# A ring of channel pairs in the mixing stages of a four-layer pairwise network on one Trainium2 core

## The reference

```
x = x + L0(gn(x));  x = x + L1(gn(x));  x = x + L2(gn(x));  x = x + L3(gn(x))

L0: a, b = sigmoid((x@Wa1+ba1)*(x@Wa2+ba2)), the same with Wb      (16 channels each)
    z = einsum('bikc,bkjc->bijc', a, b)                             (16 mixed channels)
    out = sigmoid(x@Wg+bg) * (ln(z)@Wz+bz)
L1: h = (ln(x)@pi+..)*sigmoid(ln(x)@gi+..) * mask;  a1,b1,a2,b2 = split(h, 4)
    z = concat(einsum('bikd,bjkd->bijd', a1, b1), einsum('bkid,bkjd->bijd', a2, b2))   (16 + 16)
    out = (ln(z)@po+..) * sigmoid(ln(z)@go+..)
L2: a, b = split(p_in*sigmoid(g_in), 2);  z = einsum('bikc,bjkc->bijc', a, b)          (64)
    out = (ln(z)@p_out) * sigmoid(ln(x)@g_out)
L3: left, right gated and multiplied by m[i]*m[k];  z = einsum('bkid,bkjd->bijd', left, right)  (64)
    out = (ln(z)*gate)@W_out + b_out
```

## Time and profile before

| | |
|---|---|
| median of 3 runs | 1714.95 us |
| the profiled execution | 1716.62 us |
| its span in the trace | 1714.7 us, 26817 instructions |
| PE busy | 1435.4 us (84%) |
| DVE busy | 1172.3 us (68%) |
| ACT busy | 1050.5 us (61%) |
| POOL busy | 429.0 us (25%) |
| DMA | 381.51 MB, mean 222 GB/s |

### The profile page before, as it was taken

How to read it: one execution, slowest core, us unless ns; L and a number is a source line. 1 busy time by engine, 2 the same in 40 slices (tenths; PEclk the granted TensorE clock), 3 DMA queues, 4 the chain that set the end, 5 groups by cost and what they waited for, 6 DMA issues and landing times. The chain is left out here.

```text
span 1714.7 us, 26817 instructions
## 1 busy us (share of the span) xinstructions
PE 1435.4 (84%) x9119; PEld 750.9 (44%) x9119; DVE 1172.3 (68%) x2060; ACT 1050.5 (61%) x1845; POOL 429.0 (25%) x382
## 2 busy tenths in 40 slices
PE   5796697968587697899979997998899967785987
PEld 5535432212376242133338996222233336663443
DVE  5643587179688884289957777893499956677664
ACT  4674686844234786688856666556688834444555
POOL 5400197130000594310000000792500000000665
PEclk9898899989898898999989998998899989997999
DMA  8336310026657230079987886891088878785998
GB/s 341 105 153 225 143 54 9 1 87 194 213 205 278 99 99 13 1 270 345 344 315 298 302 302 235 303 378 51 26 343 341 345 272 319 305 305 198 375 393 314
DMA packets 140872, 381.51 MB, mean 222 GB/s; under 512 B 13505, under 2 KB 13634, under 8 KB 130626
## 3 DMA queue, kind: packets, MB, share of 16 engines
q1 hardware_dynamic: 118418, 314.95, 50.4%
q10 hardware_dynamic: 22320, 64.86, 10.1%
HBM read 191.01 MB, written 188.74 MB: 221 GB/s over the span
## 5 line engine op out<-in xcount | busy, mean ns | idle before, releaser
L1350 POOL TENSOR_TENSOR xT<-xT,work 128x512 f32<-128x512 f32 x192 | 241.7, 1277 | 700.6 <-DVE work L1395 698.2
L1046 PE MATMUL bank<-work 128*128 128x256 f32 x1408 | 349.3, 401 | 59.4 <-DVE work L1112 23.9
L746 ACT ACTIVATE work<-bank,bias 128x512 f32<-128x512 f32 x448 | 286.1, 686 | 96.3 <-PE bank L645 42.0
L1046 PEld LDWEIGHTS bank<-work 128*128 128x128 f32 x1408 | 277.7, 205 | 104.5 <-DMA work<-hidden_rows 31.9
L645 PE MATMUL bank<-work,w 64*64 64x512 f32 x2048 | 257.2, 605 | 6.0 <-ACT work L742 6.0
L818 DVE SCALAR_TENSOR_TENSOR work<-bank,bias,work 128x512 f32<-128x512 f32 x320 | 236.4, 748 | 31.8 <-PE bank L645 24.2
L1069 ACT COPY work<-bank 128x512 f32<-128x512 f32 x176 | 103.3, 587 | 235.9 <-PE bank L1046 182.7
L1534 POOL TENSOR_TENSOR xT<-xT,work 128x512 f32<-128x512 f32 x64 | 80.2, 1275 | 384.4 <-ACT work L1504 384.4
L1138 DVE TENSOR_TENSOR work<-work 128x512 f32<-128x512 f32 x176 | 121.1, 688 | 71.9 <-ACT work L1069 70.5
L1395 DVE SCALAR_TENSOR_TENSOR work<-bank,bias,work 128x512 f32<-128x512 f32 x192 | 141.9, 748 | 38.2 <-ACT work L1325 22.8
L645 PEld LDWEIGHTS bank<-work,w 64*64 64x64 f32 x2048 | 84.4, 134 | 141.5 <-DVE work L818 83.0
(11 more groups left out here) (149 smaller groups left out, 2084.2 us busy)
## 6 DMA issues: line engine op xcount, KB each, us to landing
hidden_rows<-work SPq DMA_DIRECT2D x128, 512.0 KB, 3.8
work<-hidden_rows SPq DMA_DIRECT2D x60, 1024.0 KB, 7.8
products<-work ACTq DMA_DIRECT2D x88, 512.0 KB, 4.9
work<-products SPq DMA_DIRECT2D x88, 512.0 KB, 4.6
work<-gate_rows SPq DMA_DIRECT2D x64, 512.0 KB, 5.5
work<-hidden SPq DMA_DIRECT2D x18, 1024.0 KB, 8.2
work<-in_x SPq DMA_DIRECT2D x32, 512.0 KB, 4.8
gate_rows<-work SPq DMA_DIRECT2D x32, 512.0 KB, 2.7
```

What stands on the lines that cost most here:

```text
L746: nc.scalar.activation(result(t, column), GB[n % len(GB)][:, :], ACT.Sigmoid, bias=bias(name)).then_inc(gate_sb, 1)
L1046: mm = pe.matmul(ZB[c % 2][:, r * N:r * N + N], a[:, kk, rows_of(r)], x[:, kk, :], start=(kk == 0), stop=(kk == 1))
L1350: pool.tensor_tensor(columns(t), columns(t), term[:, t % RING, :], ALU.add).then_inc(x_sb, 1)
```

## The change

`make_mask` is gone, and the two calls of `mix` in layer 1 are one.

- The buffers of loads are a ring of four pairs of channels (`RING = 4`) of each operand, as large as before. The first four channels still come as single loads, operand a from SyncE's queue and operand b from ScalarE's. Every later pair is two DMAs of 512 KB (4 KB of each row at a time) on SyncE, issued when the pair four before it has been stored (issued) and its products are done.
- The stores of products move from ScalarE's queue to SyncE's, each just ahead of the load of the pair that is four later. `zs` holds `OUT` = 3, 2, 3, 4 pairs in layers 0 to 3.
- The projections return their store semaphores instead of waiting for them; SyncE and ScalarE wait for them at the start of `mix`.
- The masks of layers 1 and 3 are loaded by DMAs on ScalarE's queue at the start of `mix`, ahead of that wait, and are made by TensorE and VectorE (layer 1) or VectorE alone (layer 3).
- In layer 3 operand b's first half is scaled by VectorE and its second half by ScalarE, two channels ahead. On ScalarE this stands ahead of `out` and `square` in each step.
- `finish` and `finish_out` issue their first three gate loads before they wait for the products.

The core of the diff:

```
 project0 / project:
-            for s in range(RP):
-                sp.wait_ge(stored[s], 16 * stores * len(range(s, PAIRS, RP)))
+    return [(stored[s], 16 * stores * len(range(s, PAIRS, RP))) for s in range(RP)]
 mix:
-    LOAD = 4
+    SINGLES, RING = 4, 4
+    OUT = {0: 3, 1: 2, 2: 3, 3: 4}[layer]
...
         @block.sync
         def _(sp):
-            for c in range(LOAD):
+            def load(g):
                 for o in range(2):
-                    sp.dma_start(to_source(slots(o, 0)[:, c:c + 1, :]), source(offsets[o] + c, 1)).then_inc(single[c], 16)
-            for g in range(1, channels // LOAD):
-                if nturn == 2:
-                    at_least(sp, turn_mm, 2 * LOAD * (g - 1))
-                else:
-                    at_least(sp, z_mm, LOAD * (g - 1))
-                for o in range(2):
-                    first = offsets[o] + g * LOAD
-                    sp.dma_start(to_source(slots(o, g)), source(first, LOAD)).then_inc(landed[g % 2], 16)
+                    sp.dma_start(places(o, 2 * g, 2).rearrange("p m x -> p (m x)"),
+                                 source(o, 2 * g, 2)).then_inc(landed[g % RING], 16)
+            def store(g):
+                sp.wait_ge(z_sb, 2 * g + 2)
+                sp.dma_start(zdst[:, :, :, 2 * g:2 * g + 2, :].rearrange("w v h c x -> (v h) w (c x)"),
+                             zs[:, 2 * (g % OUT):2 * (g % OUT) + 2, :].rearrange("p c x -> p (c x)")
+                             ).then_inc(stored[g % OUT], 16)
+            wait_rows(sp)
+            for c in range(SINGLES):
+                load_single(sp, 0, c)
+            for g in range(SINGLES // 2, RING):
+                load(g)
+            for g in range(PAIRS):
+                store(g)
+                if g + RING < PAIRS:
+                    sp.wait_ge(z_mm, 2 * g + 2)
+                    load(g + RING)
...
         @block.scalar
+            def scaled_half(c):
+                if row_mask:
+                    if c == 0:
+                        act.wait_ge(mask_sb, 1)
+                    wait_loaded(act, c)
+                    x = loaded(1, c)[:, N:2 * N]
+                    nc.scalar.activation(x, x, ACT.Copy, scale=msq[:, 1:2]).then_inc(scaled, 1)
...
+            wait_rows(act)
+            for c in range(SINGLES):
+                load_single(act, 1, c)
+            for c in range(2):
+                scaled_half(c)
             for c in range(channels):
-                turned(c)
+                if c + 2 < channels:
+                    scaled_half(c + 2)
+                turned_a(c)
                 if c:
-                    finished(c - 1)
+                    out(c - 1)
+                    square(c - 1)
...
         @block.vector
-                    for kk in range(2):
-                        x = loaded(1, c)[:, kk * N:kk * N + N]
-                        dve.tensor_scalar(x, x, msq[:, kk:kk + 1], None, ALU.mult).then_inc(masked_b, 1)
+                    x = loaded(1, c)[:, 0:N]
+                    dve.tensor_scalar(x, x, msq[:, 0:1], None, ALU.mult).then_inc(masked_b, 1)
 build:
-        make_mask(core, 1, mask, mask_t)
-        mix(core, 1, 0, 16, (0, 16), (True, True), 0, 32, mask, mask_t, sums)
-        out = mix(core, 1, 1, 16, (32, 48), (False, False), 16, 32, mask, mask_t, sums)
+        out = mix(core, 1, 32, [(0, 16), (32, 48)], 16, (True, True), 32, rows, mask, mask_t, sums)
```

More of the change, by code:

```diff
@@ L573, in _ @@
                 sp.dma_start(dst, hid[:, n % OUT, :, :]).then_inc(stored[n % OUT], 16)
[L574 to L575 removed]
+    return [(s, 16 * len(range(b, PAIRS // 2, OUT))) for b, s in enumerate(stored)]
 def project(core, layer, gate_w, value_w, ogate_w, ub, gmean):
@@ L927, in mix @@
-def mix(core, layer, part, channels, offsets, turns, z_row, cz, mask, mask_t, sums):
+    return [(stored[s], 16 * stores * len(range(s, PAIRS, RP))) for s in range(RP)]
+def mix(core, layer, channels, offsets, turned, turns, cz, rows_out, mask, mask_t, sums):
     nc, bank = core.nc, core.bank
@@ L935, in mix @@
     shift, msq = core.fold[:, 11:12], core.fold[:, 8:10]
-    LOAD = 4
+    SINGLES, RING = 4, 4
+    OUT = {0: 3, 1: 2, 2: 3, 3: 4}[layer]
     X = 2 * N
[L938 to L941, removed]
+    PAIRS = channels // 2
+    masked_turn = layer == 1
+    row_mask = layer == 3
+    zs, at = core.area([2 * OUT, X], (2 if mask is None else 4) * X)
@@ L953, in mix @@
     TB = [[bank[0], bank[1]], [bank[2], bank[3]]]
     ZB = [bank[4], bank[5]]
-    with ExitStack() as ctx:
[L957 to L961, removed]
+    MB = bank[6]
@@ new lines, in mix, with source @@
+    nturn = sum(turns)
+    turns_of = lambda c: turns if c < turned else (False, False)
+    masked_load = lambda c: layer == 1 and c >= turned
+    def source(o, c, n):
+        first = offsets[c >= turned][o] + (c - turned if c >= turned else c)
+        return image[:, :, :, first:first + n, :].rearrange("w v h m x -> (v h) w (m x)")
+    with ExitStack() as ctx:
+        (mask_in, mask_mm, mask_sb, masked_a, masked_b, scaled, turn_mm, ta_sb, tb_sb, z_mm, z_sb, sq_sb, s1_sb, s2_sb, begun,
+         shifted) = core.sems(f"mix{layer}", "mask_in mask_mm mask_sb masked_a masked_b scaled turn_mm ta_sb tb_sb z_mm z_sb "
+                              "sq_sb s1_sb s2_sb begun shifted")
+        single = core.sems(f"mix{layer}", " ".join(f"single{c}" for c in range(SINGLES)))
+        landed = core.sems(f"mix{layer}", " ".join(f"in{n}" for n in range(RING)))
+        stored = core.sems(f"mix{layer}", " ".join(f"st{n}" for n in range(OUT)))
@@ L1045, in product @@
                     for kk in range(2):
-                        mm = pe.matmul(ZB[c % 2][:, r * N:r * N + N], a[:, kk, rows_of(r)], x[:, kk, :],
+                        mm = pe.matmul(ZB[c % 2][:, r * N:r * N + N], a[:, kk, rows_of(r, c)], x[:, kk, :],
                                        start=(kk == 0), stop=(kk == 1))
                 mm.then_inc(z_mm, 1)
+            if layer == 1:
+                pe.wait_ge(mask_in, 16)
+                for kk in range(2):
+                    for r in range(2):
+                        mm = pe.transpose(MB[:, kk * N + r * P:kk * N + r * P + P], mask[:, r, kk * P:kk * P + P],
+                                          core.ident[:, :])
+                mm.then_inc(mask_mm, 1)
             for c in range(channels):
@@ L1155, in _ @@
             summed(channels - 1)
-    return [(s, 16 * (channels // 4)) for s in stored]
+    return [(s, 16 * len(range(n, PAIRS, OUT))) for n, s in enumerate(stored)]
 class Roots:
@@ L1266, in _, with load_gates @@
         def _(sp):
+            def load_gates(i):
+                sp.dma_start(gate[:, i % IN, :, :].rearrange("p j t -> p (j t)"),
+                             core.gate_d[:, 2 * i * T:2 * i * T + 2 * T]).then_inc(gates_in[i % IN], 16)
+            if stored_gate:
+                for i in range(IN):
+                    load_gates(i)
             for s, n in products_out:
```

151 lines of the change are left out of this document (80 added, 71 removed).

## The result

The changed kernel takes 1663.61 us (median of 4 runs, 1662.93 to 1668.79) where the kernel before takes 1714.43 us beside it (1708.78 to 1717.31): a ratio of 0.9714, 95% interval 0.9682 to 0.9746, or 51 us faster. The forecast was 1645 in a range of 1625 to 1670: the direction and the range hold, but of 70.5 us forecast only 51 came, and nearly all that is missing belongs to one term, layer 3. The profiled execution took 1663.4 us and its span is 1661.5, which is 53.2 less than before. I split those 53.2 by stage.

What follows compares the result with a forecast made beforehand. TensorE was taken to bound layer 2, waits on bursty loads and on stores layer 3. Gains 12.5 + 18 + 1.5 + 38.5 = 70.5 us from the profiled 1716.6 give 1646.1; median 1.7 lower, called 1645, range 1625 to 1670.

Steps and rivals of the forecast that it cites:

- Layer 0, 12.5 us: Layer 0's mixing: products 2.20 us apart without load stalls save 10.3 us, the split first loads 2.2; bounds 7 and 14.
- Layer 1, 18 us: Layer 1: the mask block and earlier first loads save 6.0 us, one mixing call instead of two 12.2; bounds 13 and 21.
- the joint: Between layer 1's two mixing calls: block end, new first loads and load stalls go, saving 12.2 us.
- Layer 2, 1.5 us: Layer 2's mixing, PE full at 2.61 us per channel: only block end and split first loads gain, 0 to 3 us.
- Layer 3, 38.5 us: Layer 3's mixing: earlier start and 2.04 us per channel at 385 GB/s; 17.5 us at 331 GB/s, 49 at 419.
- It just holds: Layer 3: queued transfers of 4.1 us cover 2.2 of work and 1.5 of transfer start, so the DMA engines stay full.
- rival A: Layer 3: ScalarE's wait for a landing drains the DMA queue; 4.9 us per pair, 25 us come back, 1670; chance 0.14.
- rival B: DMA engines do better or waits overlap better: layer 3 at 419 GB/s, total gain 82 us, 1633; chance 0.15.
- The split scaling: Layer 3's operand b: VectorE loses a scaling of 0.3 us per channel, ScalarE gains one of 0.4; both faster than DMA.
- DMA share under 0.9 means A: Layer 3's sign in the changed profile: a DMA share staying under 0.9 would show rival A; near 1.0 was forecast.
- Priced at nothing, the early gates: Early gate loads of `finish` and `finish_out`: hidden by over 10 us of computing roots; worth 1 to 2 us without that cover.
- rival C: Layer 3: PE's clock, lowered after idling for loads, never gets back to 2.4 GHz; slower, 1730 us; chance 0.04.

Runs made afterwards that it cites:

- more slots: The kernel before with four pairs of product buffers in layer 3 instead of two, loads unchanged: 1712.51 us, ratio 0.9976.

## Why the prediction was right, and where it was wrong

**Layer 0, 12.5 us.** Measured 12.2 at the end of its last sum, 1.2 of them already there before the mixing. The pitch of 2.20 without a load wait is as forecast.

**Layer 1, 18 us.** Measured 16.3: the gap from the projection's last store to the first loads fell from 7.2 to 1.8 us (5.4 for 6.0), the mixing from 103.0 to 92.0 (11.0 for 12.2). The run in two calls confirms the joint, 10.7 us of mixing. (The prediction's "about 86 us" for this mixing doesn't follow from its own sum, 103.0 - 12.2 = 90.8; measured are 92.0 and, in the second trace, 89.8.)

**Layer 2, 1.5 us.** Measured 0.2: its mixing is 2.0 shorter, but the first loads came 5.6 us after the last store, where it was 3.8. In the three traces of the old code (before, halved loads, more slots) it is 3.8 each time; where the rows' stores are waited for at the start of `mix` it goes from 3.4, in the changed kernel's second trace, to 5.9. So the change made it vary; why, no run shows.

**Layer 3, 38.5 us: the term that was mis-sized.** Measured 21.0: 4.9 at the start (forecast 5.2) and 16.1 from the first load to the last sum (154.6 for 170.7; the forecast has about 137). The failed step is "It just holds", the handover: I set 4.1 us of queued transfers against 2.2 of work and 1.5 of start, a margin of 0.4, and gave rival A 0.14. (The 1.5 stands on no row.) In the handover shown, the work takes 3.2 us, from the scaling at 1440.63 to the end of the last issue at 1443.83: SyncE issues three DMAs there, and I counted two. The queued pair covers only 3.7 (1444.35), so 0.5 is left for the start of the next transfers instead of 1.5. Of the loop, 3.2 us are this work and 5.9 the median from a load's issue to its landing, 9.1 for two pairs or 4.6 per pair, against A's 4.9 in its price. The copies are 2.3 us apart in the mean, where the forecast had 2.0. The changed kernel itself spread here: its second trace has 160.3 us for this stage.

Rival A is what happened, at a smaller size, and the runs show it by cause: with the wait behind the copy, or with the scaling gone from ScalarE, layer 3 takes 132 to 133 us, below the forecast.

That leaves a second error, of the other sign: the rate. I took 385 GB/s, from 170 ns for a 4 KB piece; fed without gaps the stage moves 403 to 418 with 4 KB pieces alone, 157 to 163 ns each, near rival B's 419. With the handover cured (132.9 us), the forecast is 4 us too slow in this term. That the time fell within the range owes something to how wide the range was: its upper end, 1670, is rival A's own price, and the sum itself was 19 us too low.

**The split scaling, a half of each to two engines.** I priced its relief of VectorE as 0.3 us per channel and saw that nothing waited for it. ScalarE's scaling took 0.51 us, within my bounds and above my 0.4. It was never the duration that cost anything; it was its place, ahead of instructions for which three engines wait.

**"DMA share under 0.9 means A".** The sign failed half: the whole stage shows 0.89, but the steady part 0.95 with 344 GB/s, which looks full and isn't. By share alone one would have blamed the rate. The rate decides, beside a version that is known to be fed.

**The rule on transfer size.** The 1 MiB or more that the Trainium skill's page "DMA: Bandwidth & Descriptors" (section "Bandwidth") asks for isn't needed here, where several transfers are queued at a time: those of 512 KB carry up to 418 GB/s, and halving those of 1024 KB changed nothing that the noise would show. Its 358 GB/s is said of two cores that stream; only one does here, so no run tests it. (At that rate the prediction's sum gives 29 us, not 28.)

**Priced at nothing, the early gates.** From layer 3's last sum to the end the span has 147.5 us, was 150.8. The 3.3 may be the early gate loads, which I put at 0, or 1 to 2 us without their cover. But ten further traces with the same code behind layer 3 show 146.7 to 153.0, and the two other traces without the early loads 153.8 and 148.8, so the difference can't be told from the spread between executions. No run singled them out: open.

**The clock (rival C)** didn't come. TensorE's granted clock is 1.00 in 19 of the 20 stretches of 5 us between 1380 and 1480. It fell once, to 0.66, after TensorE had stood 2.0 us for the square (until 1470.08); after a longer stand, 2.6 us until 1433.91, it did not.

```profile
1465.00:1470.00 5.00, 3.06 (x15) 2.43 (x13) 2.39 (x6) 2.31 (x6) 0.00 (x0) 1.00 0.97 359
1470.00:1475.00 5.00, 4.92 (x15) 4.08 (x16) 3.65 (x8) 3.48 (x7) 0.00 (x0) 0.66 0.93 346
```

The sum by stage: 12.2 + 16.3 + 0.2 + 21.0 + 3.3 = 53.0 us. The stretches between these, group norms and projections, take 0.9 more and 0.3 and 0.7 less, which leaves the 53.2 that the spans differ by, but for rounding. The second trace of the changed kernel splits its 47.3 as 9.5, 18.5, 1.5, 15.4 and 2.0. So a stage differs by 1 to 6 us between two executions of one kernel, and only layer 3's shortfall of 17 and 23 us is clear of that.

## What to carry to other kernels

On an engine that runs in order, ask of each instruction that waits for a transfer what stands behind it, and whether the next transfer depends on that. If it does, the wait has closed a loop, and its length divided by the pairs under way is the pace: put the instructions that free buffers first, and the wait last. And read GB/s beside the busy share of the DMA engines: the share alone doesn't tell a full queue from a thin one.

## What was not expected of the hardware

- The DMA engines' busy share and their rate part: 344 GB/s at 0.95 and 403 at 1.02, with the same pieces in both directions. Per busy share that is 362 against 395: a piece keeps an engine busy longer in the version with fewer transfers under way. Why, no run shows.
- Moving the same scaling behind the copy made a load's landing slower (7.4 for 5.9 us) and the kernel 21 us faster.
- A VectorE sum of two SBUF operands took 0.68 us alone and 1.75 beside a multiplication on GpSimd; GpSimd's took 1.26 to 10.5 us.
